# Two bands of look-ahead for the layer norm in the first stage of a fused attention and mixture-of-experts layer

## The chip, the cores and the metric

One Trainium2 chip, and one of its cores. The metric is the device time of one execution in microseconds (us). Each kernel is run several times; a profiler records one further execution, and the rows below come from it. TensorE is PE in the rows (PEld its weight loads), VectorE is DVE, ScalarE is ACT, GpSimd is POOL, SyncE is SP. A "q" behind a name is the engine's instruction queue.

## The reference

The input x is 2 x 256 x 56 x 56. One layer is computed: a channel layer norm, a 7x7 neighbourhood attention with 8 heads and a relative bias, a residual, then a token layer norm and a mixture of 8 experts with the best 2 chosen per token. Only the first lines concern the stage that changes:

```
def _ln_c(v, eps=1e-6):
    m = jnp.mean(v, axis=1, keepdims=True)
    s = jnp.var(v, axis=1, keepdims=True)
    return (v - m) / jnp.sqrt(s + eps)
...
    xh = jnp.transpose(x, (0, 2, 3, 1))
    qkv = xh @ w_qkv.T + b_qkv
    q = qkv[0] * scale
...
    x = x + _L0_conv_ref(_ln_c(x), L0_conv_w_qkv, L0_conv_b_qkv, L0_conv_rpb, L0_conv_w_proj, L0_conv_b_proj)
```

## The kernel before

The kernel has four stages, each a block of its own that ends only when all engines have ended: `stage_a` (layer norm and q, k, v), `stage_b` (attention), `stage_c` (projection and routing) and `stage_e` (experts). The change touches `stage_a` alone.

`stage_a` goes over 6272 tokens in 14 bands of 448, each of 4 tiles of 112 tokens (`TPG`). The parity of a band, `s`, names its half of each double buffer. What one band needs:

- SyncE loads the band into `a_x` (`load`).
- VectorE computes mean and variance (`normalise`: 4 `bn_stats`, 4 `bn_aggr`), ScalarE the root (`roots`), VectorE reciprocal and normalised values `a_xn` (`scale`).
- TensorE transposes them, 8 transposes into `a_ps_t` (`transposes`, line 416). ScalarE casts them to float16, `a_xt_hi` (`high_half`, 328); VectorE keeps what the cast lost, `a_xt_lo` (`low_half`, 248).
- TensorE multiplies: four chunks of q and k into `a_ps_q` (26 products, lines 425 and 428), then v into `a_ps_v` (28 products, 437 and 440). Each value is again split: ScalarE evicts the high part (346, 348, 358), VectorE the low one (258, 260, 272).
- SyncE stores `a_o_hi`, `a_o_lo` and `a_v`, which the second stage loads.

Weights are split in the same way. The q and v biases enter the sums as one more product of `a_b_rows`, three bfloat16 parts of the bias that `bias_rows` makes on VectorE, with a constant tile. Beside all this, expert weights are loaded into `a_w_in` half an expert per band; ScalarE scales them (`w1_high`, `w1_scaled`, 333 and 336) and GpSimd splits them (`split_w1`, 383). GpSimd also issues some transfers for the attention bias.

Each engine runs its own list in a fixed order. In the step of band k the orders are:

- TensorE: wait for `xt_ok` (the low half of band k), q and k products of k, wait for `xn_ok`, transposes of k+1, wait for `v_free`, v products of k.
- ScalarE: root of k+1, evictions of q and k of band k, `high_half` of k+1, `w1_high`, two evictions of v, `w1_scaled`.
- VectorE: `normalise` of k+1, low part of chunk 0, `scale` of k+1, low parts of chunks 1 to 3, `low_half` of k+1, two low parts of v. The last step leaves out what belongs to k+1.
- SyncE: wait for `x_used`, load band k+3, wait for `w1_free` (GpSimd's split), load expert weights, wait for `qk_out`, two stores, wait for `v_out`, one store.

Ahead of the loop VectorE runs `normalise(0)`, waits for all constants (`consts`), scales the weights, runs `scale(0)`, splits the weights, runs `low_half(0)` and only then `bias_rows()`. TensorE's first product waits for `even_ok`, the end of `bias_rows`. The bands run in a hardware loop of two steps per turn, so a branch lies between every second pair of steps.

Of the kernel before, what the change touches and what calls it, by code (L numbers as in the profile page):

```python
# [15 lines left out]
B, C, H, W = 2, 256, 56, 56  # L16
# [55 lines left out]
def stage_a(nc, x, wqkv, bqk, brow, rpb, w1, ident, rpb_pad, rpb_cols, qk_hi, qk_lo, v_rows, bias, w1s):  # L72

    with ExitStack() as c:
# [3 lines left out]
        def sem(name):  # L78
            return c.enter_context(nc.semaphore(name))
# [26 lines left out]
        ps_v = c.enter_context(nc.psum_tensor("a_ps_v", [128, 2, 512], F32))  # L106

        consts = sem("a_consts")
        ident_in = sem("a_ident_in")
        scaled = sem("a_scaled")  # L110
        w_ok = sem("a_w_ok")
        x_in = [sem(f"a_x_in{i}") for i in range(2)]
        x_used = sem("a_x_used")
        stat = sem("a_stat")
        var_ok = sem("a_var_ok")
        sd_ok = sem("a_sd_ok")
        xn_ok = sem("a_xn_ok")
        t_ok = sem("a_t_ok")
        hi_ok = sem("a_hi_ok")
        xt_ok = sem("a_xt_ok")  # L120
# [38 lines left out]
        with nc.Block() as block:  # L159

            @block.sync
            def _(sp):
                def load(s, tok):
                    sp.dma_start(xg[:, s], x[bass.ds(tok, BAND), :].rearrange("(t p) c -> p t c", p=QT)
                                 ).then_inc(x_in[s], 16)

                def load_w1(s, e):
                    sp.dma_start(w1_in[:, s], w1[:, bass.ds(e, 1), s * WCH:(s + 1) * WCH
                                                 ].rearrange("p a n -> p (a n)")).then_inc(w1_ld[s], 16)

                def step(s, tok, e, left):

                    if left >= 1:
                        sp.wait_ge(x_used, s + 1)
                    if left >= 3:
                        load(1 - s, tok + 3 * BAND)
                    sp.wait_ge(w1_free, s + 1)
                    if e is not None:
                        load_w1(s, e)
                    sp.wait_ge(qk_out, s + 1)  # L180
                    sp.dma_start(qk_hi[:, :, bass.ds(tok, BAND)], o_hi[:, s]).then_inc(stored_hi[s], 16)
                    sp.dma_start(qk_lo[:, :, bass.ds(tok, BAND)], o_lo[:, s]).then_inc(stored_lo[s], 16)
                    sp.wait_ge(v_out, s + 1)
                    sp.dma_start(v_rows[bass.ds(tok, BAND), :].rearrange("(t p) c -> p t c", p=QT),
                                 v_sb[:, s].rearrange("p (t h) d -> p t (h d)", t=TPG)).then_inc(stored_v[s], 16)

                load(0, 0)
                sp.dma_start(id_a[:, :], ident).then_inc(ident_in, 16)
                sp.dma_start(w_f[:, :, :], wqkv).then_inc(consts, 16)
                sp.dma_start(b_qk[:, :], bqk).then_inc(consts, 16)  # L190
                sp.dma_start(b_f[:, :], brow.to_broadcast([128, 2 * C])).then_inc(consts, 16)
                load(1, BAND)
                for s in range(2):
                    load_w1(s, 0)
                sp.wait_ge(x_used, 1)
                sp.sem_inc(x_used, -1)
                load(0, 2 * BAND)
                for s in range(2):
                    sp.wait_ge(w1_free, s + 1)
                    load_w1(s, 1)  # L200
                sp.sem_inc(w1_free, -2)
                with sp.Fori(0, GROUPS // 2 - 2) as i:
                    for s in range(2):
                        step(s, (2 * i + s) * BAND, i + 2, 3)
                    for q in (x_used, w1_free, qk_out, v_out):
                        sp.sem_inc(q, -2)
                step(0, (GROUPS - 4) * BAND, E - 1, 3)
                step(1, (GROUPS - 3) * BAND, E - 1, 2)
                for q in (x_used, w1_free, qk_out, v_out):
                    sp.sem_inc(q, -2)  # L210
                step(0, (GROUPS - 2) * BAND, None, 1)
                step(1, (GROUPS - 1) * BAND, None, 0)

            @block.vector
            def _(dve):
                dve.memset(v_sb[:, :, :, 2 * HD:2 * HD + 2], 1.0)
                dve.memset(eps[:, :], 1e-6)
                dve.sem_inc(stored_lo[0], 16)
                dve.sem_inc(stored_lo[1], 16)
# [2 lines left out]
                def normalise(s):  # L222

                    dve.wait_ge(x_in[s], 16)
                    dve.sem_inc(x_in[s], -16)
                    for t in range(TPG):
                        last = dve.bn_stats(st6[:, s, t, :], xg[:, s, t, :])
                    last.then_inc(stat, 1)
                    dve.wait_ge(stat, 1)
                    for t in range(TPG):  # L230
                        last = dve.bn_aggr(st2[:, s, t, :], st6[:, s, t, :])
                    last.then_inc(var_ok, 1)

                def scale(s):
                    dve.wait_ge(sd_ok, 1)
                    dve.sem_inc(sd_ok, -1)
                    dve.reciprocal(rs[:, s, :], sd[:, s, :]).then_inc(stat, 1)
                    dve.wait_ge(stat, 2)
                    dve.sem_inc(stat, -2)
                    for t in range(TPG):  # L240
                        last = dve.tensor_scalar(xn[:, s, t, :], xg[:, s, t, :], st2[:, s, t, 0:1], rs[:, s, t:t + 1],
                                                 ALU.subtract, ALU.mult)
                    last.then_inc(xn_ok, 1)

                def low_half(s):
                    dve.wait_ge(hi_ok, 1)
                    dve.sem_inc(hi_ok, -1)
                    dve.tensor_tensor(xt_lo[:, s], ps_t[:, :, 0:BAND], xt_hi[:, s], ALU.subtract).then_inc(xt_ok, 1)

                def step(s, last):  # L250
                    if not last:
                        normalise(1 - s)
                    dve.wait_ge(stored_lo[s], 16)
                    dve.sem_inc(stored_lo[s], -16)
                    for m in range(4):
                        dve.wait_ge(qh_ok, m + 1)
                        if m < 2:
                            low = dve.tensor_tensor(kept(o_lo, s, m), chunk(ps_q, m), kept(o_hi, s, m), ALU.subtract)
                        else:
                            low = dve.scalar_tensor_tensor(kept(o_lo, s, m), chunk(ps_q, m), b_qk[:, m:m + 1],  # L260
                                                           kept(o_hi, s, m), ALU.add, ALU.subtract)
                        if m == 0 and not last:
                            scale(1 - s)
                        if m == 1 and not last:
                            low.then_inc(x_used, 1)
                    low.then_inc(qk_out, 1)
                    dve.sem_inc(qh_ok, -4)
# [25 lines left out]
                    last.then_inc(even_ok, 1)  # L293

                normalise(0)
                dve.wait_ge(consts, 48)
                dve.tensor_scalar(w_f[:, :, 0:C], w_f[:, :, 0:C], HD ** -0.5, None, ALU.mult).then_inc(scaled, 1)
                scale(0)
                dve.wait_ge(scaled, 1)
                dve.tensor_copy(w_hi[:, 0], w_f[:, 0]).then_inc(x_used, 1)  # L300
                dve.tensor_copy(w_hi[:, 1], w_f[:, 1]).then_inc(scaled, 1)
                dve.wait_ge(scaled, 2)
                dve.tensor_tensor(w_lo[:, :, :], w_f[:, :, :], w_hi[:, :, :], ALU.subtract).then_inc(w_ok, 1)
                low_half(0)
                bias_rows()
                with dve.Fori(0, GROUPS // 2 - 1):
                    for s in range(2):
                        step(s, False)
                step(0, False)
                step(1, True)  # L310
                for s in range(2):
                    dve.wait_ge(stored_lo[s], 16)

# [1 line left out]
            def _(act):  # L315
# [2 lines left out]
                    act.sem_inc(stored_v[s], 16)  # L318

                def roots(s):  # L320
                    act.wait_ge(var_ok, 1)
                    act.sem_inc(var_ok, -1)
                    act.activation(sd[:, s, :], st2[:, s, :, 1], ACT.Sqrt, bias=eps[:, :]).then_inc(sd_ok, 1)

                def high_half(s):
                    act.wait_ge(t_ok, 1)
                    act.sem_inc(t_ok, -1)
                    act.copy(xt_hi[:, s], ps_t[:, :, 0:BAND]).then_inc(hi_ok, 1)
# [6 lines left out]
                def w1_scaled(s):  # L335
                    act.activation(w1_in[:, s], w1_in[:, s], ACT.Copy, scale=WSCALE).then_inc(w1_hi, 1)

                def step(s, e, last):
                    if not last:
                        roots(1 - s)  # L340
                    act.wait_ge(stored_hi[s], 16)
                    act.sem_inc(stored_hi[s], -16)
                    for m in range(4):
# [17 lines left out]

                roots(0)
                high_half(0)
                for s in range(2):
                    w1_high(s, 0)
                    w1_scaled(s)
                act.wait_ge(consts, 48)
                with act.Fori(0, GROUPS // 2 - 1) as i:
                    for s in range(2):
                        step(s, i + 1, False)  # L370
                step(0, E - 1, False)
                step(1, E - 1, True)
                for s in range(2):
                    act.wait_ge(stored_hi[s], 16)
                    act.wait_ge(stored_v[s], 16)
# [31 lines left out]
            def _(pe):  # L407
# [1 line left out]
                parts = ((w_hi, xt_hi), (w_hi, xt_lo), (w_lo, xt_hi))  # L409

                def transposes(s):
                    pe.wait_ge(xn_ok, 1)
                    pe.sem_inc(xn_ok, -1)
                    for k in range(KC):
                        for t in range(TPG):
                            last = pe.transpose(ps_t[:, k, t * QT:(t + 1) * QT], xn[:, s, t, k * 128:(k + 1) * 128],
                                                id_a[0:QT, 0:QT])
                    last.then_inc(t_ok, 1)
# [1253 lines left out]
```

## Time and profile before

| | us |
|---|---|
| median of 3 runs | 1417.42 |
| lowest, highest | 1414.5, 1421.49 |
| the profiled execution, its own time | 1420.68 |
| span of the instructions in it | 1418.9 |
| DVE busy in the span | 892.0 (63%) |
| PE busy in the span | 1168.9 (82%) |
| mean granted clock of TensorE | 0.931 of full speed |

The profiled execution lies 3.3 us above the median. Busy shares are means over four stages with different limits, so the first stage is read by itself: it lasts from the start to about 197 us, when the first instructions of the second stage run.

### The profile page before, as it was taken

How to read it: one execution, taken by the hardware profiler on the slowest of the kernel's cores; microseconds unless marked ns; L12 is line 12 of the kernel's file. 1: busy time of each engine (PE TensorE's matmuls, PEld its weight loads, DVE VectorE, ACT ScalarE, POOL GpSimd, SP SyncE). 2: the span in 40 equal slices, each digit the busy share in tenths (PEclk: the TensorE clock that was granted, in tenths of full speed). 3: DMA queues.
4: the chain of work that ended last, by engine and by line, in shares of the span. 5: the costliest groups of instructions: out<-in, count | busy, mean ns of one | idle time of the engine just before them, and what ended most of it. 6: DMA issues, size and time to landing. Idle time of an engine off the chain costs nothing. (4 is left out here: it accounts for less than half of the span.)

```text
span 1418.9 us, 38575 instructions
## 1 busy us (share of the span) xinstructions
PE 1168.9 (82%) x12144; PEld 982.0 (69%) x12145; DVE 892.0 (63%) x3140; ACT 654.8 (46%) x1329; POOL 729.9 (51%) x792
## 2 busy tenths in 40 slices
PE   2888828898888947888179999999999999999995
PEld 1656528788887836777157777777777777777774
DVE  6766628888888835766345555565555555565652
ACT  2555528888888825455033333333333333333331
POOL 5111126666666601766625555555555555555555
PEclk9999968999999978777589999999999999999998
DMA  7666668767767547987512222222222222222222
GB/s 164 195 195 203 181 173 187 191 183 186 182 182 192 151 132 238 305 292 231 166 32 47 40 45 46 46 46 46 42 45 43 46 39 45 46 46 46 46 43 27
DMA packets 152179, 169.79 MB, mean 120 GB/s; under 512 B 14287, under 2 KB 143967, under 8 KB 151719
## 3 DMA queue, kind: packets, MB, share of 16 engines
q1 hardware_dynamic: 115958, 132.10, 33.5%
q0 software_dynamic: 21920, 29.38, 12.5%
q10 hardware_dynamic: 14240, 7.55, 2.1%
q8 instruction: 32, 0.52, 0.2%
q14 instruction: 29, 0.23, 0.1%
HBM read 108.36 MB, written 65.49 MB: 123 GB/s over the span
## 5 line engine op out<-in xcount | busy, mean ns | idle before, releaser
L1462 PE MATMUL e_ps_h<-e_xt,w1s 128*128 128x256 f16 x2688 | 321.1, 275 | 29.3 <-DVE e_g_lo L1535 25.1
L1511 ACT ACTIVATE e_gf<-e_ps_h,keep_b 128x256 f32<-128x256 f32 x448 | 203.6, 475 | 266.8 <-PE e_ps_h L1462 266.4
L1477 PE MATMUL e_ps_y<-w2s,e_g_hi 128*128 x1792 | 297.8, 273 | 18.4 <-issue 18.3
L1462 PEld LDWEIGHTS e_ps_h<-e_xt,w1s 128*128 x2688 | 246.3, 98 | 95.2 <-issue 55.9
L1477 PE MATMUL e_ps_y<-w2s,e_g_lo 128*128 x896 | 244.2, 273 | 0.0
L825 POOL TENSOR_TENSOR b_p<-b_s,b_p 128x392 f16<-128x392 f32 x196 | 182.8, 932 | 118.3 <-DVE b_p L723 114.4
L1415 POOL DMA_INDIRECT out<-e_y,e_xg x112 | 181.0, 1616 | 78.4 <-POOLq L1412 44.5
L1535 DVE TENSOR_TENSOR e_g_lo<-e_gf,e_g_hi 128x256 f16<-128x256 f32 x448 | 201.0, 449 | 15.5
L1477 PEld LDWEIGHTS e_ps_y<-w2s,e_g_hi 128*128 128x128 f16 x1792 | 175.0, 98 | 49.7 <-issue 27.8
L1533 DVE CAST e_g_hi<-e_gf 128x256 f16<-128x256 f32 x448 | 138.7, 310 | 53.9 <-ACT e_gf L1511 53.9
L780 ACT ACTIVATE b_s<-b_s,b_neg_max 128x196 f32<-128x196 f32 x392 | 158.4, 455 | 19.7 <-DVE b_neg_max L704 19.3
L1549 DVE SCALAR_TENSOR_TENSOR e_y_f<-e_ps_y,keep_b 128x512 f32<-128x512 f32 x56 | 38.7, 692 | 186.1 <-DVEq L1548 179.4
L1149 POOL DMA_INDIRECT slots<-c_xs,c_slot x98 | 104.0, 1061 | 100.5 <-DVE c_slot L1241 70.5
L1409 POOL TENSOR_SCALAR e_y<-e_y_f,e_gate 128x256 f32<-128x256 f32 x112 | 105.0, 947 | 97.7 <-POOLq L1404 95.2
L704 DVE CUSTOM_DVE_ANT_1 b_s<-b_ps_s,bias 128x196 f32<-128x196 f32 x392 | 131.6, 360 | 31.5 <-PE b_ps_s L630 24.0
L630 PE MATMUL b_ps_s<-b_k,b_q 128*128 128x196 f16 (+1 forms) x784 | 114.6, 269 | 35.6 <-PEq L626 25.8
L644 PE MATMUL b_ps_p<-b_ident,b_p 128*128 128x128 f16 x1568 | 122.5, 222 | 22.8 <-ACT b_pt L804 22.2
L804 ACT COPY b_pt<-b_ps_p 98x512 int32<-98x512 int32 x196 | 113.4, 579 | 42.6 <-PE b_ps_p L644 37.5
L1511 ACT ACT_TABLE_LOAD x28 | 35.9, 1283 | 207.0 <-PE e_ps_h L1462 207.0
L644 PEld LDWEIGHTS b_ps_p<-b_ident,b_p 128*128 128x128 f16 x1568 | 97.3, 99 | 37.8 <-ACT b_pt L804 34.3
L662 PE MATMUL b_ps_o<-b_v,b_pt 98*128 98x66 f16 (+1 forms) x2352 | 104.5, 193 | 0.6 <-PEq L655 0.4
L630 PEld LDWEIGHTS b_ps_s<-b_k,b_q 128*128 128x128 f16 (+1 forms) x784 | 75.7, 137 | 37.5 <-issue 35.8
(143 smaller groups left out, 1719.7 us busy)
## 6 DMA issues: line engine op xcount, KB each, us to landing
b_v<-v_rows SPq DMA_DIRECT2D x196, 99.5 KB
e_xg<-slots SPq DMA_DIRECT2D x56, 273.0 KB, 2.8
b_k<-qk_hi SPq DMA_DIRECT2D x56, 196.0 KB
a_w_in<-in_w SPq DMA_DIRECT2D x16, 512.0 KB, 3.9
c_w_in<-in_w SPq DMA_DIRECT2D x16, 512.0 KB, 6.3
v_rows<-a_v SPq DMA_DIRECT2D x14, 455.0 KB, 6.7
a_x<-in_x SPq DMA_DIRECT2D x14, 448.0 KB, 6.6
qk_hi<-a_o_hi SPq DMA_DIRECT2D x14, 448.0 KB, 4.6
```

The source lines that it names most:

```text
L630: mm = pe.matmul(ps_s[:, j % 4, u * KEYS:(u + 1) * KEYS], q[0:rows, s, hp].rearrange("p h (q t) -> p t (h q)", t=COLS)[:, t, :], k[0:rows, ...
L644: last = pe.transpose(ps_p[:, j % 2, m * LANES:(m + 1) * LANES], p16[:, j % 4, half * K2 + u * KEYS + n * CK:][:, 0:128], id_b[:, :])
L704: dve.tensor_tensor_reduce(out=s_sb[:, j % 4, u * KEYS:(u + 1) * KEYS].rearrange("p (r w) -> p r w", w=KCOL), in0=ps_s[:, j % 4, u * KEYS: ...
L780: act.activation(p, p, ACT.Exp, bias=neg_max[:, j % 4, u:u + 1], scale=-1.0).then_inc(p_ok, 1)
L804: act.copy(pt_sb[:, ev % 4, :, :].rearrange("p m q -> p (m q)").bitcast(I32), ps_p[0:CK, ev % 2, :].bitcast(I32)).then_inc(pt_ok, 1)
L825: pool.tensor_tensor(p16[:, j % 4, K2:2 * K2], s_sb[:, j % 4, :], p16[:, j % 4, 0:K2], ALU.subtract).then_inc(lo_ok, 1)
L1415: pool.indirect_dma_start(out=out, out_offset=bass.IndirectOffsetOnAxis(ap=xg[:, j, h, TAIL:TAIL + 1], axis=0), in_=y_sb[:, s, h, :], in_o ...
L1462: mm = pe.matmul(ps_h[:, hc % 4, 0:ST], w1s[:, bass.ds(e, 1), w, a:a + 128].rearrange("p a n -> p (a n)"), xt[:, s, :, 2 * p + k, :], star ...
L1477: mm = pe.matmul(ps_y[:, s, h * C:(h + 1) * C], g[:, s, hc, h * 128:(h + 1) * 128], w2s[:, bass.ds(e, 1), w, a:a + C].rearrange("p a n -> ...
L1511: act.activation(gf[:, hc % 4, :], ps_h[:, hc % 4, 0:ST], ACT.Gelu, bias=b1_sb[:, bass.ds(e * HC + hc, 1)], scale=1.0 / WSCALE).then_inc(g ...
L1533: dve.tensor_copy(g_hi[:, s, hc, :], gf[:, hc % 4, :]).then_inc(hi_ok, 1)
L1535: dve.tensor_tensor(g_lo[:, s, hc, :], gf[:, hc % 4, :], g_hi[:, s, hc, :], ALU.subtract).then_inc(gs_ok, 1)
```

## The change

Five things change in `stage_a`.

1. In the step of band k, VectorE and ScalarE now run `normalise`, `roots` and `scale` for band k+2 in place of k+1. `high_half`, `low_half` and the transposes stay at k+1. The last two steps have no look-ahead.
2. SyncE loads band k+4 in place of k+3, into the buffer of the step's own parity, behind the same wait at the same place. Ahead of the loop two such loads are issued in place of one.
3. The signals `stat`, `var_ok`, `sd_ok` and `xn_ok` exist once per parity.
4. Ahead of the loop VectorE's order becomes `normalise(0)`, `bias_rows()`, `scale(0)`, scaling and splitting of the weights, `low_half(0)`, `normalise(1)`, `scale(1)`. ScalarE's order becomes `roots(0)`, `high_half(0)`, `roots(1)`, the first expert weights.
5. The load of the bias row `a_b_f` has a signal of its own, `b_in`, and is issued ahead of the weights. The fill of `a_v` with ones is done in two halves, the second after `scale(1)`.

The diff, cut to its core (the others of the renamed signals, and the calls of the same form, are left out):

```
@@ sync
-                def step(s, tok, e, left):
-                    if left >= 1:
+                def step(s, tok, e, more):
+                    if more:
                         sp.wait_ge(x_used, s + 1)
-                    if left >= 3:
-                        load(1 - s, tok + 3 * BAND)
+                        load(s, tok + 4 * BAND)
...
                 load(0, 0)
                 sp.dma_start(id_a[:, :], ident).then_inc(ident_in, 16)
+                sp.dma_start(b_f[:, :], brow.to_broadcast([128, 2 * C])).then_inc(b_in, 16)
                 sp.dma_start(w_f[:, :, :], wqkv).then_inc(consts, 16)
                 sp.dma_start(b_qk[:, :], bqk).then_inc(consts, 16)
-                sp.dma_start(b_f[:, :], brow.to_broadcast([128, 2 * C])).then_inc(consts, 16)
                 load(1, BAND)
                 for s in range(2):
                     load_w1(s, 0)
-                sp.wait_ge(x_used, 1)
-                sp.sem_inc(x_used, -1)
-                load(0, 2 * BAND)
+                for s in range(2):
+                    sp.wait_ge(x_used, s + 1)
+                    load(s, (2 + s) * BAND)
+                sp.sem_inc(x_used, -2)
@@ vector
-                dve.memset(v_sb[:, :, :, 2 * HD:2 * HD + 2], 1.0)
+                dve.memset(v_sb[:, 0, :, 2 * HD:2 * HD + 2], 1.0)
...
-                def step(s, last):
-                    if not last:
-                        normalise(1 - s)
+                def step(s, ahead, last):
+                    if ahead:
+                        normalise(s)
...
-                        if m == 0 and not last:
-                            scale(1 - s)
-                        if m == 1 and not last:
+                        if m == 0 and ahead:
+                            scale(s)
+                        if m == 1 and ahead:
                             low.then_inc(x_used, 1)
...
                 normalise(0)
-                dve.wait_ge(consts, 48)
+                dve.wait_ge(b_in, 16)
+                bias_rows()
+                scale(0)
+                dve.wait_ge(consts, 32)
                 dve.tensor_scalar(w_f[:, :, 0:C], w_f[:, :, 0:C], HD ** -0.5, None, ALU.mult).then_inc(scaled, 1)
-                scale(0)
...
                 low_half(0)
-                bias_rows()
+                normalise(1)
+                scale(1)
+                dve.memset(v_sb[:, 1, :, 2 * HD:2 * HD + 2], 1.0).then_inc(x_used, 1)
@@ scalar
-                def step(s, e, last):
-                    if not last:
-                        roots(1 - s)
+                def step(s, e, ahead, last):
+                    if ahead:
+                        roots(s)
...
                 roots(0)
                 high_half(0)
+                roots(1)
@@ tensor
                 def transposes(s):
-                    pe.wait_ge(xn_ok, 1)
-                    pe.sem_inc(xn_ok, -1)
+                    pe.wait_ge(xn_ok[s], 1)
+                    pe.sem_inc(xn_ok[s], -1)
```

## Rows read from the trace of the kernel before

**Rows 1.** Windows: one stretch, busy us of each engine, PEclk, DMA share, GB/s

```profile
26.80:187.70 160.90, 133.82 (x860) 96.48 (x860) 108.68 (x266) 85.30 (x138) 33.09 (x24) 0.95 0.62 187
```

**Rows 2.** Waits from 26 to 195 us: total us, times, longest

```profile
PE a_ps_t L416 <- PEq L413: 25.7, 12, 2.4
```

**Rows 3.** Timeline of PE and of q products: start us, us, instruction [idle before]

```profile
36.96 0.35 PE L425 MATMUL a_ps_q<-a_even,a_b_rows 128*128 128x448 bf16 x1
...
66.21 0.96 PE L416 MATMUL a_ps_t<-a_ident,a_xn 112*128 112x112 f32 x8 [1.95 <-PEq L413]
...
166.90 0.35 PE L425 MATMUL a_ps_q<-a_even,a_b_rows 128*128 128x448 bf16 x1
...
178.22 0.35 PE L425 MATMUL a_ps_q<-a_even,a_b_rows 128*128 128x448 bf16 x1
```

**Rows 4.** Timeline of VectorE: one band, and the stage's last instruction

```profile
52.93 0.62 DVE L258 TENSOR_TENSOR a_o_lo<-a_ps_q,a_o_hi 128x448 f16<-128x448 f32 x1 [0.88 <-ACT a_o_hi L346]
...
55.62 1.27 DVE L260 SCALAR_TENSOR_TENSOR a_o_lo<-a_ps_q,a_b_qk,a_o_hi 128x448 f16<-128x448 f32 x2
57.45 1.09 DVE L248 TENSOR_TENSOR a_xt_lo<-a_ps_t,a_xt_hi 128x896 f16<-128x896 f32 x1 [0.56 <-DVEq L247]
58.77 0.69 DVE L272 TENSOR_TENSOR a_v<-a_ps_v,a_v 112x512 f16<-112x512 f32 x1 [0.23 <-ACT a_v L358]
59.99 0.69 DVE L272 TENSOR_TENSOR a_v<-a_ps_v,a_v 112x512 f16<-112x512 f32 x1 [0.53 <-ACT a_v L358]
...
63.82 0.62 DVE L258 TENSOR_TENSOR a_o_lo<-a_ps_q,a_o_hi 128x448 f16<-128x448 f32 x1 [0.88 <-ACT a_o_hi L346]
...
187.01 0.69 DVE L272 TENSOR_TENSOR a_v<-a_ps_v,a_v 112x512 f16<-112x512 f32 x1 [0.83 <-ACT a_v L358]
```

**Rows 5.** Timeline of ScalarE: the cast of the transposed band

```profile
56.40 0.91 ACT L328 CAST a_xt_hi<-a_ps_t 128x896 f16<-128x896 f32 x1 [2.01 <-ACTq L327]
```

**Rows 6.** Windows: two bands, PEclk and DMA share in each

```profile
59.10:70.00 10.90, 8.95 (x53) 6.32 (x51) 7.74 (x20) 5.62 (x9) 2.13 (x1) 0.87 0.69 202
70.00:82.90 12.90, 10.59 (x76) 7.98 (x75) 8.40 (x21) 6.68 (x11) 2.12 (x1) 0.98 0.64 196
```

**Rows 7.** Timeline of all engines: the start of the stage

```profile
1.71 0.42 SPq L189 DMA_DIRECT2D a_w<-in_wqkv  x1
...
10.65 0.43 DVE L297 TENSOR_SCALAR a_w<-a_w 128x512 f32<-128x512 f32 x1 [4.16 <-DMA a_b_f<-in_brow]
10.99 0.17 DVE L237 RECIPROCAL a_rs<-a_sd 112x4 f32<-112x4 f32 x1
...
12.61 0.55 DVE L300 CAST a_w_hi<-a_w 128x768 f16<-128x768 f32 x1
...
15.44 1.06 ACT L333 ACTIVATE w1s<-a_w_in 128x1024 f16<-128x1024 f32 x1
...
16.70 0.34 DVE L285 TENSOR_SCALAR a_b_f<-a_b_f 128x256 f32<-128x256 f32 x1
...
18.29 1.04 ACT L336 ACTIVATE a_w_in<-a_w_in 128x1024 f32<-128x1024 f32 x1
18.31 5.27 DVE L290 COPY a_b_rows<-a_b_part 32x512 bf16<-32x512 bf16 x1
19.22 4.21 POOL L383 TENSOR_TENSOR w1s<-a_w_in,w1s 128x1024 f16<-128x1024 f32 x2
...
26.16 0.31 DVE L290 COPY a_b_rows<-a_b_part 32x512 bf16<-32x512 bf16 x1
...
26.82 0.53 PE L425 MATMUL a_ps_q<-a_even,a_b_rows 128*128 128x448 bf16 x1 [12.30 <-PEq L422]
...
29.63 0.53 ACT L346 CAST a_o_hi<-a_ps_q 128x448 f16<-128x448 f32 x1 [0.88 <-PE a_ps_q L428]
```

**Rows 8.** DMA issues from 0 to 12 us: KB, us from issue to landing

```profile
a_w<-in_wqkv SPq DMA_DIRECT2D x1, 768.0 KB, 4.9
```

**Rows 9.** DMA issues from 48 to 59 us

```profile
qk_lo<-a_o_lo SPq DMA_DIRECT2D x1, 448.0 KB, 6.9
```

More of the change, by code:

```diff
@@ L108, in stage_a @@
         consts = sem("a_consts")
+        b_in = sem("a_b_in")
         ident_in = sem("a_ident_in")
@@ L113, in stage_a @@
         x_used = sem("a_x_used")
[L114 to L117, printed above, removed]
+        stat = [sem(f"a_stat{i}") for i in range(2)]
+        var_ok = [sem(f"a_var_ok{i}") for i in range(2)]
+        sd_ok = [sem(f"a_sd_ok{i}") for i in range(2)]
+        xn_ok = [sem(f"a_xn_ok{i}") for i in range(2)]
         t_ok = sem("a_t_ok")
@@ L203, in _ @@
                     for s in range(2):
-                        step(s, (2 * i + s) * BAND, i + 2, 3)
+                        step(s, (2 * i + s) * BAND, i + 2, True)
                     for q in (x_used, w1_free, qk_out, v_out):
                         sp.sem_inc(q, -2)
-                step(0, (GROUPS - 4) * BAND, E - 1, 3)
-                step(1, (GROUPS - 3) * BAND, E - 1, 2)
-                for q in (x_used, w1_free, qk_out, v_out):
+                step(0, (GROUPS - 4) * BAND, E - 1, False)
+                step(1, (GROUPS - 3) * BAND, E - 1, False)
+                for q in (w1_free, qk_out, v_out):
                     sp.sem_inc(q, -2)
-                step(0, (GROUPS - 2) * BAND, None, 1)
-                step(1, (GROUPS - 1) * BAND, None, 0)
+                step(0, (GROUPS - 2) * BAND, None, False)
+                step(1, (GROUPS - 1) * BAND, None, False)
             @block.vector
             def _(dve):
-                dve.memset(v_sb[:, :, :, 2 * HD:2 * HD + 2], 1.0)
+                dve.memset(v_sb[:, 0, :, 2 * HD:2 * HD + 2], 1.0)
                 dve.memset(eps[:, :], 1e-6)
@@ L227, in normalise @@
                         last = dve.bn_stats(st6[:, s, t, :], xg[:, s, t, :])
-                    last.then_inc(stat, 1)
-                    dve.wait_ge(stat, 1)
+                    last.then_inc(stat[s], 1)
+                    dve.wait_ge(stat[s], 1)
                     for t in range(TPG):
                         last = dve.bn_aggr(st2[:, s, t, :], st6[:, s, t, :])
-                    last.then_inc(var_ok, 1)
+                    last.then_inc(var_ok[s], 1)
                 def scale(s):
[L235 to L239, printed above, removed]
+                    dve.wait_ge(sd_ok[s], 1)
+                    dve.sem_inc(sd_ok[s], -1)
+                    dve.reciprocal(rs[:, s, :], sd[:, s, :]).then_inc(stat[s], 1)
+                    dve.wait_ge(stat[s], 2)
+                    dve.sem_inc(stat[s], -2)
                     for t in range(TPG):
@@ L242, in scale @@
                                                  ALU.subtract, ALU.mult)
-                    last.then_inc(xn_ok, 1)
+                    last.then_inc(xn_ok[s], 1)
                 def low_half(s):
@@ L304, in _ @@
                 low_half(0)
-                bias_rows()
+                normalise(1)
+                scale(1)
+                dve.memset(v_sb[:, 1, :, 2 * HD:2 * HD + 2], 1.0).then_inc(x_used, 1)
                 with dve.Fori(0, GROUPS // 2 - 1):
                     for s in range(2):
-                        step(s, False)
-                step(0, False)
-                step(1, True)
+                        step(s, True, False)
+                step(0, False, False)
+                step(1, False, True)
                 for s in range(2):
@@ L320, in roots @@
                 def roots(s):
-                    act.wait_ge(var_ok, 1)
-                    act.sem_inc(var_ok, -1)
-                    act.activation(sd[:, s, :], st2[:, s, :, 1], ACT.Sqrt, bias=eps[:, :]).then_inc(sd_ok, 1)
+                    act.wait_ge(var_ok[s], 1)
+                    act.sem_inc(var_ok[s], -1)
+                    act.activation(sd[:, s, :], st2[:, s, :, 1], ACT.Sqrt, bias=eps[:, :]).then_inc(sd_ok[s], 1)
                 def high_half(s):
@@ L366, in _ @@
                     w1_scaled(s)
-                act.wait_ge(consts, 48)
+                act.wait_ge(consts, 32)
                 with act.Fori(0, GROUPS // 2 - 1) as i:
                     for s in range(2):
-                        step(s, i + 1, False)
-                step(0, E - 1, False)
-                step(1, E - 1, True)
+                        step(s, i + 1, True, False)
+                step(0, E - 1, False, False)
+                step(1, E - 1, False, True)
                 for s in range(2):
```

## The prediction

> **What bounds the kernel now.** I read the windows by stage first, then the waits inside the first stage, then the timeline of one band engine by engine, then the start. Only the first stage is touched, and a block closes it, so the question is when it ends. From the first product at 26.8 us to VectorE's last instruction at 187.7 us it takes 160.9 us, in which PE is busy 133.8 and VectorE 108.7 [rows 1]. No engine is full, so a loop of waits sets the pace.
>
> The waits show one that ends on TensorE: before the transposes it stands still 12 times, 25.7 us in all, 2.1 us a time [rows 2]. It waits for the normalised values, which VectorE makes in the same band after its first low part. This late start passes on: ScalarE idles 2.01 us ahead of the cast of the transposed band [rows 5]; VectorE then idles 0.56 us ahead of the low half, and 0.23 and 0.53 us ahead of the two low parts of v, whose products stand behind the transposes [rows 4]. The loop closes through `low_half`, then v, `normalise`, root, eviction, low part, `scale`, transposes. A band takes 10.89 us (52.93 to 63.82) [rows 4], or 11.32 where the hardware loop branches (166.90 to 178.22) [rows 3].
>
> There is a second loss. Product starts 1 to 12 lie at 36.96 and 166.90, 129.9 us for 11 bands [rows 3]. Six of 10.89 and five of 11.32 would be 121.9, so 8 us are missing. The windows say where: the granted clock has a mean of 0.87 in the band that ends at 70.0, so part of it ran at 1.2 in place of 2.4 GHz, after TensorE had been idle 1.95 us, and the next band takes 12.9 us in place of 11.3 [rows 3, 6].
>
> **The change in the steady bands.** With `scale` two bands ahead, `a_xn` of k+1 is ready a whole step before TensorE asks for it. TensorE goes from q and k straight to the transposes: its band is 8.95 us, the busy time of a band without idle [rows 6]. No instruction is added to a step and none removed; the order on VectorE and ScalarE is as before, only the buffer is another. So ScalarE still waits for the root before it evicts chunk 0, and the 0.88 us of VectorE ahead of its first low part stay [rows 4]; I give nothing for them.
>
> What goes on VectorE is 0.56 + 0.23 + 0.53 = 1.32 us [rows 4], if the casts are early enough. They are: q and k products start at the end of `low_half`, transposes are done about 6.1 us later, the cast 7.1; VectorE reaches the next `low_half` after v, `normalise`, root and low parts, about 8.5 us later. The second v sum is evicted about 9.9 us later, VectorE wants it at 10.1: just in time. 10.89 - 1.32 = 9.57; instructions with no wait between them start some 0.08 us before the end of the one ahead (two of 0.67 in 1.27 [rows 4]), so I take 9.5. VectorE is then the bound, 0.5 us over TensorE's 8.95, and it is VectorE's waits on ScalarE that are late next. Bounds: 9.3 with all overlaps, 10.2 if half of the waits come back. The branch adds 0.43 in every second band. 11 x 9.5 + 5.5 x 0.43 = 106.9 us against 129.9: **23.0 saved**, of which 8 is the clock.
>
> Step 12 has no look-ahead any more; its root, `normalise` and `scale` are gone, and it runs at TensorE's 8.95 in place of 11.32: **2.4 saved**. From product start 13 at 178.22 to the end at 187.70 nothing changes [rows 3, 4].
>
> **Transfers.** The loads and stores are as many and as large, and stand at the same places of SyncE's list; load k+4 has as long until its use as load k+3 had. What changes is the density. A band's transfers take 0.69 of 10.9 or 0.64 of 12.9 us [rows 6], about 7.9 us of all engines; in 9.7 us that is 0.81. The nearest deadline is the low store: it takes 6.9 us to land [rows 9] and is issued about 4.2 us after the end of v, so it lands at 11.1, and its buffer is written again at 9.7 + 3.1 = 12.8. 1.7 us are left where there were about 3. Hidden, as I see it, but this is the cover to watch.
>
> **The start.** Here the chain is serial on VectorE. Today the first low half ends at 16.70, `bias_rows` runs from 16.70 to 26.47, and the products begin at 26.82. One copy of it took 5.27 us where its twin took 0.31; it ends with GpSimd's two splits, at 19.22 + 4.21 = 23.43 [rows 7]. Moved, `bias_rows` runs long before those splits: 9.77 - 4.96 = 4.8 us. The SBUF page of the Trainium skill ("SBUF — State Buffer", section "Who interferes with whom") says why this could be so: VectorE in a 2-port mode and GpSimd hold the shared ports exclusively, and the later one blocks fully. The trace agrees with this one copy; the same rule would let the splits, now at 24 to 28 us, block the first `scale` of the loop, at most about 1 us.
>
> The bias row's landing is unknown. The weights, 1280 KB queued with what is ahead, landed at 1.71 + 4.9 = 6.6 [rows 7, 8]; the bias row, last of the constants, at 10.65 [rows 7]. Now it is behind 512 KB only, yet its 256 KB were slow. I take the middle, 8.6; the bounds are 6.6 and 10.65.
>
> From there: `bias_rows` 4.8, `scale(0)` 1.6 (10.99 to 12.61), weight scaling 0.5, splitting of the weights and first low half 4.1 (12.61 to 16.70): `low_half(0)` ends at 19.6, and TensorE starts, 7.2 us earlier than today. But this isn't what counts, since ScalarE can't evict: `roots(1)` now stands ahead of its first expert weights and waits for `normalise(1)`, 2.3 us after the low half (an estimate from the 3.14 us between 60.68 and 63.82 [rows 4], less an eviction and the queue), and the four expert operations take 3.9 (15.44 to 19.33 [rows 7]). With 0.3 for the root of band 2, chunk 0 is evicted at 19.6 + 2.3 + 3.9 + 0.3 = 26.1 against 29.63. From there to product start 1 VectorE needs 0.56, then 3.95 as in a steady band, then 1.09: 5.6 us against 7.3 today. Product start 1 at 31.7 in place of 36.96: **5.3 saved**. The second expert weights are loaded later too and may cost ScalarE up to 1 us in step 0.
>
> **Sum.** 5.3 + 23.0 + 2.4 = 30.7. The profiled execution would go from 1420.7 to 1390.0; its median stands 3.3 lower, 1417.4 - 30.7 = **1386.7**.
>
> **Rivals.**
>
> The clock still falls. In favour: TensorE still idles 0.5 to 1 us a band. Against: that is less than half of today's idle, and with it only every second band fell. Price: 12.9 - 11.3 is what a fall cost; TensorE's band would be 8.95 + 1.9 = 10.9, 1.3 over VectorE's, in 5 or 6 bands: 7.5 us back, 1394. [...]
>
> Transfers become the bound. In favour: 0.81 occupied, 1.7 us of slack. Against: the engines have gaps in every band. If the stores set the pace at 10.3 us, 12 x 0.7 = 8 come back, 1395.
>
> The start gains nothing: the bias row lands no earlier, or a VectorE instruction again waits 5 us for GpSimd. Price 2 to 5, 1389 to 1392.
>
> The change doesn't do what it says: VectorE's waits stay, because something else than the transposes holds ScalarE. Then only the start and step 12 gain, about 6: 1411. Against: the list of ScalarE shows nothing between the evictions and the cast.
>
> Slower: the clock falls for good. If TensorE's short idles kept it at 1.2 GHz, a band would take 17.9 us and the stage some 80 us more. It decides from a third of the time at 1.2 GHz, where TensorE's band passes 11.8 us. Against: today's mean is 0.95 with more idle [rows 1].
>
> **How the numbers follow.** Chances: forecast 0.60, clock falls 0.12, transfers 0.11, start gains nothing 0.10, change without effect 0.04, slower 0.03. The measurement can't tell less than about 0.5% (7 us) from no change. Range: below, the bias row at 6.6 and bands of 9.3 give 4 more, and the median of a few runs another 3 or 4: 1379. Above, the transfers and the clock, 1395, and part of both together: 1401. Faster 0.93, same 0.04, slower 0.03.
>
> **What would show it.** Right: TensorE's wait ahead of line 416 is gone from the bands; it waits instead about 0.5 us ahead of line 425; bands of 9.5 to 9.9 us; the copy at line 290 takes 0.3 us each time; first product near 19.6, first eviction near 26; clock 1.0 from 40 us on; the second stage 30 us earlier, and as long as before. Wrong: VectorE waits ahead of 248 or 272 as before, or ahead of 258 by more than 0.9 us (stores); the copy or another VectorE instruction lasts as long as a split; a later stage changes its length.

## The result, and the profile after

| | before | after |
|---|---|---|
| median | 1419.45 us (4 runs) | 1382.91 us (4 runs, 1381.08 to 1384.75) |
| ratio | | 0.9746, 95% interval 0.9723 to 0.977 |
| span of the profiled execution | 1418.9 us | 1382.9 us |
| VectorE's last low part of v | 187.01 | 153.36 |
| second stage begins | 197.15 | 163.33 |

36.0 us of span are gone, 33.8 of them before the second stage begins. The forecast was 30.7 us, to a median of 1386.7, with a range of 1379 to 1401. The median before is 2.0 us above the 1417.42 from which the forecast was taken, with one run more. The lines that answer to [rows 2 to 5], from the timeline of the kernel after (line numbers have moved by a few: 431 is the q product, 422 the transposes, 249 the low half, 273 the low part of v). First TensorE:

```profile
17.85 0.53 PE L431 MATMUL a_ps_q<-a_even,a_b_rows 128*128 128x448 bf16 x1 [2.51 <-PEq L428]
...
30.23 0.35 PE L431 MATMUL a_ps_q<-a_even,a_b_rows 128*128 128x448 bf16 x1 [1.98 <-PEq L428]
...
65.04 0.93 PE L422 MATMUL a_ps_t<-a_ident,a_xn 112*128 112x112 f32 x8
69.76 0.35 PE L431 MATMUL a_ps_q<-a_even,a_b_rows 128*128 128x448 bf16 x1 [0.72 <-PEq L428]
...
79.05 0.35 PE L431 MATMUL a_ps_q<-a_even,a_b_rows 128*128 128x448 bf16 x1 [0.38 <-PEq L428]
...
135.82 0.35 PE L431 MATMUL a_ps_q<-a_even,a_b_rows 128*128 128x448 bf16 x1 [0.38 <-PEq L428]
...
144.56 0.35 PE L431 MATMUL a_ps_q<-a_even,a_b_rows 128*128 128x448 bf16 x1
```

Nothing stands in brackets behind the transposes: the wait of 1.95 us is gone. TensorE now waits ahead of the q products, 0.38 and 0.72 us in turn. VectorE, one band (from 64.66 to 73.94):

```profile
64.66 0.62 DVE L259 TENSOR_TENSOR a_o_lo<-a_ps_q,a_o_hi 128x448 f16<-128x448 f32 x1 [0.87 <-ACT a_o_hi L351]
...
68.53 1.08 DVE L249 TENSOR_TENSOR a_xt_lo<-a_ps_t,a_xt_hi 128x896 f16<-128x896 f32 x1
69.53 1.28 DVE L273 TENSOR_TENSOR a_v<-a_ps_v,a_v 112x512 f16<-112x512 f32 x2
...
73.94 0.63 DVE L259 TENSOR_TENSOR a_o_lo<-a_ps_q,a_o_hi 128x448 f16<-128x448 f32 x1 [0.87 <-ACT a_o_hi L351]
```

The three waits of 0.56, 0.23 and 0.53 us are gone, the one of 0.87 stays. The band takes 9.28 us, the next one, with the branch, 9.65 (73.94 to 83.59). Of the clock the windows tell this (same columns as [rows 6]):

```profile
20.00:40.00 20.00, 18.02 (x113) 12.16 (x112) 17.29 (x44) 14.18 (x22) 15.08 (x19) 0.91 0.74 166
40.00:60.00 20.00, 18.64 (x132) 13.28 (x130) 16.56 (x42) 12.62 (x22) 4.26 (x2) 1.00 0.92 291
60.00:80.00 20.00, 18.77 (x130) 13.23 (x131) 16.65 (x42) 13.34 (x22) 4.25 (x2) 1.00 0.81 251
```

TensorE is at 2.4 GHz from 40 us on; the windows up to 140 us all show 1.00. The timeline of all engines at the start, with a surprise in it:

```profile
7.06 0.29 DVE L286 TENSOR_SCALAR a_b_f<-a_b_f 128x256 f32<-128x256 f32 x1 [0.62 <-DMA a_b_f<-in_brow]
...
11.49 0.28 DVE L291 COPY a_b_rows<-a_b_part 32x512 bf16<-32x512 bf16 x1
...
20.33 1.38 DVE L242 TENSOR_SCALAR a_xn<-a_x,a_st,a_rs 112x256 f32<-112x256 f32 x4 [0.15 <-DVEq L240]
...
22.03 4.22 POOL L389 TENSOR_TENSOR w1s<-a_w_in,w1s 128x1024 f16<-128x1024 f32 x2 [2.78 <-POOLq L388]
...
23.78 0.95 ACT L351 CAST a_o_hi<-a_ps_q 128x448 f16<-128x448 f32 x2
...
25.18 2.19 DVE L242 TENSOR_SCALAR a_xn<-a_x,a_st,a_rs 112x256 f32<-112x256 f32 x4 [0.15 <-DVEq L240]
...
34.99 2.14 POOL L389 TENSOR_TENSOR w1s<-a_w_in,w1s 128x1024 f32 x1
...
35.27 2.99 DVE L242 TENSOR_SCALAR a_xn<-a_x,a_st,a_rs 112x256 f32<-112x256 f32 x4 [0.15 <-DVEq L240]
```

The bias row lands at 7.06, the stall of 5.27 us is gone, the first eviction is at 23.78 in place of 29.63. But two of the scales (line 242) take 2.19 and 2.99 us where the others take 1.38, and beside both runs a split of GpSimd. In the second, one of the four instructions lasts 2.02 us (35.27 to 37.29) and ends 0.16 us after the split. The second costs a whole band: start 1 to start 2 is 10.89 us (30.23 to 41.12).

### The profile page after: what moved, and what is told of

Same layout as the page of the kernel before. It is cut to its first block and busy times, and to the rows that moved or that the text cites. A ratio compares the mean times of both kernels' runs of the same rounds, so it can differ in the third digit from the quotient of the medians.

```text
span 1382.9 us, 38574 instructions
## 1 busy us (share of the span) xinstructions
PE 1157.8 (84%) x12144; PEld 970.9 (70%) x12145; DVE 886.6 (64%) x3141; ACT 654.1 (47%) x1329; POOL 729.0 (53%) x792
## 5 line engine op out<-in xcount | busy, mean ns | idle before, releaser
L1555 DVE SCALAR_TENSOR_TENSOR e_y_f<-e_ps_y,keep_b 128x512 f32<-128x512 f32 x56 | 38.7, 692 | 185.9 <-DVEq L1554 179.6
```

## The experiments

Ratios are to the kernel before, measured beside it on the same chip; "first stage" is the end of VectorE's last instruction in it (187.70 before, 154.05 after).

**e1: the start alone.** The kernel before, with

```
+ b_f loaded ahead of w_f, on its own signal b_in
  normalise(0)
+ dve.wait_ge(b_in, 16); bias_rows(); scale(0); dve.wait_ge(consts, 32)
...
  low_half(0)
- bias_rows()
```

> The kernel before, with the new start alone (bias row loaded ahead of the weights, bias_rows ahead of the first scale); no look-ahead. Theory (the start is worth what brings the first eviction forward): the weights of w1 are not behind a second root here, so the first eviction is held by ScalarE's four w1 operations (to about 20.2) and then by root and product, about 20.6 in place of 29.6; 9 us gained, less up to 1.6 us if the first scale of the loop meets GpSimd's splits at 19 to 23.5 and is blocked by them; bands stay at 10.9 and 11.3 with the clock falling in every second one. Time 8 us lower, 1411, ratio 0.994. Rival (parts add up, the start gave 6.7 us in the changed kernel): 1413. Rival (the stalled copy is not due to the splits): one VectorE instruction lasts 5 us again and 4 us are gained.

1408.22 us, ratio 0.9931 (0.9906 to 0.9956); first eviction at 20.49, first stage 178.89, 8.8 us shorter. So the start alone is worth more than the 6.7 us that it brings in the changed kernel. The scale of step 0 took 2.26 us beside the splits (18.82 to 23.05).

**e2: the look-ahead alone.** The changed kernel with the bias row loaded last of the constants, and `bias_rows()` between `low_half(0)` and `normalise(1)`.

> The changed kernel with the old start: bias row loaded last of the constants, bias_rows behind the first low half. Theory: the products begin at about 21.7, normalise(1) ends at 23.4, w1 operations at 27.6, first eviction at 27.9 in place of 23.8; bands as in the changed kernel (9.29 and 9.63). 4 us above the changed kernel: 1387, ratio to before 0.977. The copy that took 5.27 us is not near a split of GpSimd here (they come after 24 us): 0.3 us if the splits caused it, about 0.8 us if GpSimd's issuing of transfers (to 19.2) did. Rival (start and look-ahead depend on each other, the start carries most): 1395 or more.

1385.97 us, ratio 0.9768 (0.974 to 0.9795); first eviction at 27.54, first stage 157.82, 29.9 us shorter than before. Gains of 8.8 and 29.9 make 38.7, together they give 33.6. The bands save the same in e2 as in the changed kernel (33.98 to 139.59 is 105.6 us for 11), so the 5.1 us lie in the start, where two things overlap. The stall of the copy is gone in e2 too, though `bias_rows` was not moved: `roots(1)` now stands ahead of the w1 operations, so the splits come later. And that same place of `roots(1)` holds the first eviction at 23.78 where e1 had 20.49. No run here separates the two. The copy of the bias part, again at 18 us and again beside GpSimd's issuing of transfers, but with the splits still 7 us off (timeline of e2):

```profile
15.05 4.62 POOL L398 DMA_DIRECT2D rpb_cols<-rpb_pad  x8 [5.64 <-DMA rpb_pad<-a_pad]
...
18.12 0.37 DVE L291 COPY a_b_rows<-a_b_part 32x512 bf16<-32x512 bf16 x1
...
25.79 4.21 POOL L389 TENSOR_TENSOR w1s<-a_w_in,w1s 128x1024 f16<-128x1024 f32 x2 [6.11 <-POOLq L388]
```

0.37 us: the 5.27 us of the kernel before did not come from the issues and belonged to the splits (it ended 0.15 us after them, 23.58 against 23.43). So moving `bias_rows` is one way to be rid of the stall, and the look-ahead by itself was another. What the new start adds to the look-ahead is 3.8 us (157.82 to 154.05).

**e3: the clock by itself.** The kernel before, with work in TensorE's wait:

```
+ for n in range(8):
+     pe.matmul(ps_t[:, 0, 0:BAND], w_hi[:, 0, 0:128], xt_hi[:, s, 0, :], start=True, stop=True)
  transposes(1 - s)
```

> The kernel before, with eight more products of 0.19 us (results overwritten) in TensorE's wait ahead of the transposes, in every band. Theory (8 us of the gain are the clock, and the clock falls because of that wait): granted clock 1.0 from 40 to 180 us, bands of 10.9 and 11.3 with none of 12.9, first stage 8 us shorter, 1411.5, ratio 0.9944. Rival (the clock falls for another reason, such as the transposes, or a fall costs nothing in sum): bands of 12.9 stay or the time is unchanged, 1419.

1409.84 us, ratio 0.995 (0.9931 to 0.997). The windows show full clock, where [rows 6] had 0.87:

```profile
40.00:60.00 20.00, 18.68 (x127) 12.64 (x126) 14.68 (x39) 10.61 (x19) 4.25 (x2) 1.00 0.63 200
60.00:100.00 40.00, 38.33 (x253) 25.36 (x251) 28.57 (x74) 22.12 (x38) 8.51 (x4) 1.00 0.68 199
```

Product starts lie 10.89 and 11.25 us apart with none of 12.9: starts 1 to 12 take 121.6 us (38.63 to 160.24) in place of 129.9. The first stage is 6.7 us shorter although TensorE does more. The first band grew by 1.7 us, since there TensorE had no wait that the eight products could fill.

**e4: what bounds the bands now.** The changed kernel with ScalarE's root behind chunk 0:

```
- if ahead: roots(s)
  act.wait_ge(stored_hi[s], 16)
  ...
  for m in range(4):
      ...
+     if m == 0 and ahead: roots(s)
```

> The changed kernel, with ScalarE's root moved behind its eviction of chunk 0. Theory (VectorE is the bound, and 0.87 us of its band is the wait for root and eviction): that wait goes, TensorE's 8.75 us become the bound, 9.46 to 8.8 in 11 bands, 7 us less than the changed kernel: 1376, ratio to before 0.969. Rival (TensorE or the transfers already bound the bands): 1382 to 1383. Rival (the wait comes back elsewhere, stores land too late for a band of 8.8): a gain of 3 or less.

1376.71 us, ratio 0.9706 (0.9683 to 0.9729), 5.2 us less in the first stage. The timeline of VectorE in it, with its next wait:

```profile
77.48 0.69 DVE L273 TENSOR_TENSOR a_v<-a_ps_v,a_v 112x512 f16<-112x512 f32 x1 [0.53 <-ACT a_v L363]
78.97 1.41 DVE L228 BATCH_NORM_STATS2 a_st<-a_x 112x6 f32<-112x256 f32 x4 [0.80 <-DVEq L226]
...
80.71 0.59 DVE L259 TENSOR_TENSOR a_o_lo<-a_ps_q,a_o_hi 128x448 f16<-128x448 f32 x1
```

The wait of 0.87 us is gone ahead of line 259, and 0.53 us ahead of the last low part of v has come back in every second band: TensorE, whose v products feed it, has the pace. Product starts are 8.75 and 9.25 us apart. The theory had 8.8 in every band and so 7 us; the bands with the branch stayed 0.45 us above that.

**e5: the late split.** The changed kernel, with the bias transfers issued four at a time behind the splits of steps 0 to 3 (`split_w1(s, e)`, then two of the eight rows), in place of all 16 ahead of step 0's split.

> The changed kernel, with GpSimd's 16 transfers of the attention bias issued four at a time behind the splits of steps 0 to 3, in place of all ahead of step 0's split. Theory (the scale of step 1 took 2.99 us in place of 1.38 because that split began late, at 35.0, and held VectorE's second port): the split runs at 30.6 to 32.7, the scale takes 1.38, the band is 9.3 in place of 10.9; 1.6 us less, 1381.3. Rival (the scale is slow for another reason, such as landing loads): it stays at 2.99 us wherever the split is.

1382.24 us, ratio 0.9755 (0.9725 to 0.9786), which can't be told from the changed kernel. Its timeline (GpSimd, then VectorE) answers the question: the split of step 0 now comes early, and the scale of step 1 is free.

```profile
31.19 2.13 POOL L389 TENSOR_TENSOR w1s<-a_w_in,w1s 128x1024 f16<-128x1024 f32 x1 [4.49 <-issue]
...
35.72 1.38 DVE L242 TENSOR_SCALAR a_xn<-a_x,a_st,a_rs 112x256 f32<-112x256 f32 x4 [0.15 <-DVEq L240]
```

Start 1 to start 2 is 9.28 us (30.68 to 39.96) in place of 10.89.

**e6 and e7: more work for VectorE, more for TensorE.** In e6 VectorE makes the low part of chunk 2 once more, into a spare tile; in e7 TensorE has three more products at the head of each band.

> The changed kernel, with one more VectorE instruction of 0.6 us per band (the low part of chunk 2 once more, into a tile that nobody reads). Theory (VectorE is the bound of the bands): each of 12 bands 0.6 us longer, 9.9 and 10.2, 7 us in all: 1390. Rival (TensorE or the transfers are the bound): hidden, 1383 to 1384.

> The changed kernel, with three more products of 0.19 us (results overwritten) at the head of each band. Theory (VectorE is the bound; TensorE has 0.38 and 0.73 us to spare): TensorE's band is 9.32, the two-band period of 18.9 stays, and only the last two bands get longer, by 1.1 us: 1384. Rival (TensorE is the bound): 14 times 0.57 us, 8 us, 1391.

e6: 1389.7 us, ratio 0.981 (0.9781 to 0.984). 0.6 us a band on VectorE came through in full: bands of 9.88 and 10.23, 7.2 us in the first stage. e7: 1385.21 us, ratio 0.9784 (0.9758 to 0.9809). 8 us of products came through with 3.2 us (first stage 157.30): bands of 9.31 and 10.1. So VectorE is the bound of the bands without the branch, where three products cost 0.02 us. In the bands with the branch both engines are: e6 made them 0.6 us longer, and e7 0.45 of its 0.57 us. VectorE's timeline in e7 shows why TensorE's wait of 0.72 us was no slack there; the last low part of v now waits again for TensorE's v products, through ScalarE's cast:

```profile
99.95 0.69 DVE L273 TENSOR_TENSOR a_v<-a_ps_v,a_v 112x512 f16<-112x512 f32 x1 [0.39 <-ACT a_v L363]
```

**e8, e9 and e12: putting it together.** All three have e4's root. e8 also has e5's transfers and, on ScalarE, the first half of the w1 operations ahead of `roots(1)`. e9 has the transfers in fours behind each of the first four splits, so that the first pair is pulled apart. e12 is e4 with e5's transfers.

> The changed kernel with the root behind chunk 0, the bias transfers spread over four steps, and ScalarE's first half of the w1 operations ahead of its second root. Theory: the scales of steps 0 and 1 take 1.38 us in place of 2.42 and 3.51, and the first eviction no longer waits for ScalarE; 3.7 us less than with the root alone, 1373, ratio to before 0.968. Rival (the denser bands run into late stores or into TensorE, so that nothing more is gained): 1376 to 1377.

> The changed kernel with the root behind chunk 0, and GpSimd's bias transfers in fours behind each of its first four splits, so that the first pair of splits is pulled apart; ScalarE's start as in the changed kernel. Theory (a split that runs during a scale blocks it): first split 22.2 to 24.3 ends before the scale of step 0 (25.1), the second runs from 26.5, after it; scales of steps 0 and 1 and the one ahead of the loop all take 1.38 us; 1.0 + 2.1 us less than with the root alone: 1373.6, ratio 0.969. Rival (only the late split of step 1 matters, or issuing transfers blocks the scale just as much): 1375 or more, with a scale over 2 us in step 0 or 1.

> The changed kernel with the root behind chunk 0 and the bias transfers in fours behind the splits of steps 0 to 3; ScalarE's start and the first two splits as in the changed kernel. Theory: the scale of step 0 still meets the second split (2.4 us), that of step 1 is free (1.38 in place of 3.51): 2.1 us less than with the root alone, ratio to before 0.969, 1374.6 on a chip where before has 1417.4. Rival (no gain that can be told from the root alone): 0.9706.

e8: 1375.01 us, ratio 0.971 (0.9689 to 0.9732). e12: 1377.52, ratio 0.9719 (0.9702 to 0.9736). Neither can be told from e4, nor can the 1.4 us by which e12's first stage (147.53) is shorter than e4's (148.89). e9 ran on a chip where the kernel before takes 1436.47: 1400.33, ratio 0.9753 (0.9725 to 0.9781), a loss against e4; its first stage takes 152.33 against 148.89. Both misses begin with the same thing, a scale that meets a split. In e8 the first splits moved onto the scale ahead of the loop (timeline of GpSimd and VectorE):

```profile
19.65 2.14 POOL L390 TENSOR_TENSOR w1s<-a_w_in,w1s 128x1024 f16<-128x1024 f32 x1
...
20.59 4.19 DVE L242 TENSOR_SCALAR a_xn<-a_x,a_st,a_rs 112x256 f32<-112x256 f32 x4 [0.15 <-DVEq L240]
...
22.19 2.12 POOL L390 TENSOR_TENSOR w1s<-a_w_in,w1s 128x1024 f16<-128x1024 f32 x1 [0.40 <-POOLq L389]
```

and in e9 the second split moved behind transfers and onto the scale of step 0 (same view):

```profile
24.13 2.25 POOL L402 DMA_DIRECT2D bias<-rpb_cols  x4
...
24.98 4.69 DVE L242 TENSOR_SCALAR a_xn<-a_x,a_st,a_rs 112x256 f32<-112x256 f32 x4 [0.15 <-DVEq L240]
...
26.40 2.14 POOL L389 TENSOR_TENSOR w1s<-a_w_in,w1s 128x1024 f16<-128x1024 f32 x1
```

In e8 this cost at start 1 (31.66 against e4's 30.43) about what the free scale of step 1 gave back. In e9 it left TensorE idle for 4.19 us ahead of start 1, at 32.52; the clock then fell (mean of 0.66 from 34 to 40 us) and the band took 11.49 us against e4's 10.57. In e9 one instruction carries the whole hold, as the group of line 242 in this stretch of e9 shows (ns, least/median/most of four):

```profile
L242 DVE TENSOR_SCALAR a_xn<-a_x,a_st,a_rs x4: 400/401/3718, 25.0 to 29.3; 112x256 f32<-112x256 f32 x4
```

It is the first of the four, from 24.98 to 28.70, and it too ends 0.16 us after the split (28.54).

**e10: the changed kernel again**, on the chip of e9.

> The changed kernel once more, beside the last one on the same chip: 1382 to 1384, and its later stages within 2 us of 1219.6; if those scatter by 2 us or more between executions of the same code, the 2.2 us by which they were shorter than in the kernel before are no effect of the change.

1405.84 us, ratio 0.9775 (0.974 to 0.9809). The absolute time missed, as this chip is slower: the steady bands are as long as ever (start to start 9.28 and 9.64), the later stages take 1241.9 us in place of 1219.6. On the other chips the stages behind the first, whose code is the same in all of these kernels, took 1214.0 to 1221.8 us. The one fall of the clock stands elsewhere in e10: not near 31 us but behind an idle of 1.99 us ahead of start 2 (41.36), and the band that begins there took 10.43 us in place of 9.72:

```profile
40.00:46.00 6.00, 4.64 (x16) 2.08 (x17) 4.22 (x13) 1.73 (x4) 2.13 (x1) 0.72 1.04 330
```

This settles a rival for the long band of step 1. There the scale of 2.99 us and the fall near 31 us came together in the changed kernel, and in e5 neither came. In e10 the band of step 1 had the scale of 2.99 us at the full clock (1.00 from 28 to 40 us) and took 10.89 us all the same: it is the scale.

**e11: does a split hold VectorE before its row begins?** In e9 the first instruction of the scale was held, which began at 24.98, and so was the copy of the kernel before, which began at 18.31 [rows 7], both ahead of the split's row and beside issues.

> The changed kernel, with the bias transfers in halves: 8 issued behind the split of step 0 (33 to 37.5 us), 12 ahead of the split of step 1 though its data is ready at 41 (41 to 48, the split from 48), 12 later. The scale of step 1 (35.7) then runs beside issues with no split behind them, the scale of step 2 (45.4) beside issues with a ready split behind them. If a split that stands ready behind issues already holds VectorE off (as in the kernel before at 18.3 to 23.6 and in the run before this one at 25.0 to 29.6): about 1.4 us in step 1, over 4 us, to the split's end, in step 2. Rival (only a split at work blocks): 1.4 us in both. Rival (issuing blocks by itself): over 3 us in step 1 as well.

One run, 1384.93 us. The timeline of GpSimd, with the split ready at 41.2:

```profile
41.18 6.63 POOL L401 DMA_DIRECT2D bias<-rpb_cols  x12 [3.15 <-ACT a_w_in L341]
47.82 2.15 POOL L389 TENSOR_TENSOR w1s<-a_w_in,w1s 128x1024 f16<-128x1024 f32 x1
```

The scale of step 1 took 1.38 us, that of step 2 1.44 (from 45.17). Neither issuing nor a ready split behind it holds VectorE off in general; the theory falls. (The late split costs elsewhere: the first stage of e11 takes 158.26 us.) What is left is that the two held instructions began 0.91 us (the copy) and 1.42 us (e9) ahead of the split's row, and unheld would have been done 0.6 and 1.0 us ahead of it; here the scale was done 1.2 us ahead of it. Rows of GpSimd are rough; that the hold begins up to about 1 us ahead of the row would fit. It can't be so for every split: in the changed kernel the scale ahead of the loop was done at 21.71, 0.32 us ahead of a split (22.03) before which GpSimd had stood idle for 2.78 us, and took 1.38. Both early holds came at a split directly behind issues. No run isolates it.

## Why the prediction was right, and where its sizes were off

**The wait and its consequences: right.** The transposes wait no more, VectorE's three waits went with it, the 0.87 us stayed (and e4 took them). The bound moved to VectorE: e6 shows it, and e7 that in every second band TensorE is a bound as well, which the prediction, with 0.5 us between them, did not have.

**Bands: 24.3 us saved, 23.0 forecast.** Starts 1 to 12 are 30.23 and 135.82, 105.6 us against 129.9. The term was mis-sized twice, in opposite directions, so its small error is in part luck. 10.89 went to 9.28, 1.6 us in place of 1.4: each wait that goes gives back an overlap of 0.09 us too, three times, and I had counted 0.07 in all. And 1.6 us were lost in step 1, where the scale met a split.

**The clock: right.** I had 8 us of the 23 for it; e3 gives 7.9 in the median, and 8.3 between starts 1 and 12 (6.7 net in the first stage). The rival in which it goes on falling is out: in the profiled execution one fall is left, near 31 us, after the idle 1.98 us ahead of start 1, and in e10 one at 40 to 46. In that rival's price a fall is put at 1.9 us, where its own rows give 12.9 - 11.3 = 1.6.

**The start: 6.7 us saved, 5.3 forecast.** The bias row landed at 7.06, near the early bound (8.6 taken). This early landing, the lucky side of a middle value, is 1.5 us of the gain. From there to the first eviction it took 16.7 us (17.5 forecast). From the eviction to start 1 it took 6.45, not 5.6, since the scale of step 0 took 2.19 us. The step that failed is "at most about 1 us" for the splits: it held for step 0 (0.8 us), but I had moved only the first pair. The bias transfers behind them end at 34.97, so the split of step 0 waits its turn and lands on the scale of step 1. With that a sign that I had put down under wrong came true, a VectorE instruction that lasts about as long as a split: 2.02 against 2.14 us. The 4.8 us for the moved `bias_rows` is right as the length of the stall, but e2 shows that the stall would have gone without the move. The page that I named, "SBUF — State Buffer" of the Trainium skill, section "Who interferes with whom", counts `tensor_scalar` among the instructions that can take the shared ports; the trace agrees: the four instructions of a scale were together held for 0.8 to 3.3 us in every run where a split was at work for more than 0.3 us of them (2.18 to 4.69 us long), and took 1.38 to 1.45 us elsewhere. `bn_stats`, also from SBUF, is not held: it ran beside a split in nearly every band of the changed kernel and took 1.41 us for four (1.40 where no split was near, from 17.62).

**Step 12: 2.6 us saved, 2.4 forecast.** 144.56 - 135.82 = 8.74 us. From start 13 to the end nothing changed, as forecast: 9.49 us against 9.48.

**Transfers: right.** No wait of an engine on a store or a load is left in the bands; the low store landed 5.3 us after its issue, and the transfer engines were occupied for 0.81 of the bands (60 to 80 us), as forecast.

**Not forecast: 2.2 us in the later stages** (1221.75 to 1219.57). Their code did not change, and between executions they range from 1214.0 to 1221.8 us (e10). That is no effect of the change that these runs could show.

## What to carry to other kernels

When an in-order engine waits in the middle of its step, work out whose lateness is passed on: here 2.1 us on TensorE were 1.6 us on VectorE and, through the clock, another 0.7 per band. Once the look-ahead is in, read the new bound's own waits in the same view; moving one instruction (e4) gave 5 to 6 us more. And when a side engine's work moves in time, look at what it lands on: here VectorE's SBUF copy and scale stood still until GpSimd's split was done, while `bn_stats` did not, and two re-orderings (e8, e9) gained nothing or lost where a scale met a split again. And run each half of a change by itself: e2 showed that one cost was being paid off twice.

## What was not expected of the hardware

- The `tensor_scalar` of 112x256 float32, which starts every 0.33 us when it is free (four in 1.38, each 0.40 long), is held by a GpSimd split as the 16-bit copy is: one instruction of 2.02 us (after, step 1) and one of 3.72 us (e9) among neighbours of 0.40.
- In the kernel before, TensorE's waits were 1.95 us in one band and 2.3 to 2.4 us in the next. The clock fell behind the shorter one (0.50 from 68 to 70 us) and not behind the longer (1.00 from 79 to 84 us). The length of the last wait alone doesn't decide it.
- The load that broadcasts 2 KB to 128 partitions landed 5.3 us after its issue (issued at 1.71) with 512 KB queued ahead, 8.0 us with 1282 KB ahead.
- Chips differ by 1.3% on the kernel before (1417 and 1436 us). For the changed kernel the two profiled executions show where: 22.3 of 23.7 us lie in the later stages (1241.9 against 1219.57).
